# Attention with 16-feature heads: output in four quadrants of one PSUM bank, and one stage's TensorE, VectorE and ScalarE programs written out without a loop

## The reference, cut to what matters

```
# first layer (stage "Aatt"): causal, 16 heads
att = einsum('bhqd,bhkd->bhqk', q, k) / sqrt(16)
att = where(tril, att, -1e9);  att = softmax(att)
o   = einsum('bhqk,bhkd->bhqd', att, v)          # then @ W_proj + b_proj

# third layer (stage "Catt"): every query sees every key, with a bias per distance
att = einsum('bhqd,bhkd->bhqk', q, k) / sqrt(16) + compute_bias(rel_emb)
att = softmax(att)
o   = einsum('bhqk,bhkd->bhqd', att, v)          # then @ Wo
```

## Time and profile before

| | us |
|---|---|
| median of the runs | 7962.52 (three runs, 7954.46 to 7972.70) |
| the profiled execution, its own time | 7959.56 |
| its span in the profile | 7957.9 |
| from the start of `Aatt`'s products to its end, about | 280 to 1045 |
| from the start of `Catt`'s products to its end, about | 3150 to 4345 |

### The profile page before, as it was taken

How to read it: one execution, slowest core, us unless ns; L and a number is a source line. 1 busy time by engine, 2 the same in 40 slices (tenths; PEclk the granted TensorE clock), 3 DMA queues, 4 the chain that set the end, 5 groups by cost and what they waited for, 6 DMA issues and landing times. The chain is left out here.

```text
span 7957.9 us, 122287 instructions
## 1 busy us (share of the span) xinstructions
PE 6620.0 (83%) x30596; PEld 3410.1 (43%) x30596; DVE 4763.3 (60%) x12029; ACT 2802.6 (35%) x6066; POOL 1320.0 (17%) x779
## 2 busy tenths in 40 slices
PE   6799958989987966989988357996997788898979
PEld 2333334655455533222222244333554445544555
DVE  5655547733763634877775764996334675347635
ACT  0255524712462200555554111552110256124611
POOL 1110106100610003000000000551001441006100
PEclk9899989999998987999999678998998899999989
DMA  5322244542455256222221322113322345324541
GB/s 176 106 60 58 56 118 147 185 141 60 146 173 171 77 204 192 67 68 63 60 68 48 107 84 75 37 36 115 75 64 70 118 154 169 123 78 151 174 144 55
DMA packets 930584, 850.14 MB, mean 107 GB/s; under 512 B 240136, under 2 KB 786912, under 8 KB 929952
## 3 DMA queue, kind: packets, MB, share of 16 engines
q1 hardware_dynamic: 500624, 522.99, 23.0%
q10 hardware_dynamic: 429568, 323.08, 13.1%
HBM read 503.10 MB, written 346.00 MB: 107 GB/s over the span
## 5 line engine op out<-in xcount | busy, mean ns | idle before, releaser
L1243 ACT ACTIVATE Catt_E<-Catt_t 128x512 f32<-128x512 f32 x1024 | 577.6, 596 | 505.3 <-DVE Catt_t L1206 307.9
L1180 DVE CUSTOM_DVE_ANT_0 Catt_S<-Catt_s,Catt_win 128x1024 f32<-128x1024 f32 x512 | 620.8, 1214 | 5.9 <-DMA Catt_win<-skewed 3.7
L1180 DVE CUSTOM_DVE_ANT_0 Aatt_S<-Aatt_s,Aatt_win 128x128 f32<-128x128 f32 (+7 forms) x512 | 377.1, 756 | 303.8 <-PE Aatt_s L1110 297.7
L1160 PE MATMUL Catt_o<-Catt_E,Catt_V 128*32 128x256 f32 (+1 forms) x3840 | 549.5, 405 | 0.0
L1243 ACT ACTIVATE Aatt_E<-Aatt_t 128x512 f32<-128x512 f32 (+3 forms) x768 | 354.7, 489 | 326.8 <-PE Aatt_t L1142 251.5
L1206 DVE TENSOR_TENSOR Catt_t<-Catt_t,Catt_near 128x256 f32<-128x256 f32 (+2 forms) x640 | 281.7, 456 | 268.1 <-PE Catt_t L1139 234.6
L1139 PE MATMUL Catt_t<-Catt_Q,Catt_K 123*128 123x512 bf16 x1024 | 328.8, 389 | 92.8 <-ACT Catt_E L1243 73.4
L1110 PE MATMUL Catt_s<-Catt_K,Catt_Q 96*128 96x512 bf16 x1024 | 325.3, 401 | 23.4 <-DMA Catt_K<-k_parts 12.3
L1160 PE MATMUL Aatt_o<-Aatt_E,Aatt_V 128*32 128x256 f32 (+2 forms) x2304 | 323.8, 388 | 0.0
L1160 PEld LDWEIGHTS Catt_o<-Catt_E,Catt_V 128*32 128x32 f32 x3840 | 180.5, 110 | 272.9 <-issue 185.6
L2336 PE MATMUL scan_cum<-scan_X,scan_upto 128*128 128x512 f32 x512 | 265.8, 609 | 25.1 <-DVE scan_X L2405 23.7
(11 more groups left out here) (721 smaller groups left out, 14605.8 us busy)
## 6 DMA issues: line engine op xcount, KB each, us to landing
moe_cb<-c_s SPq DMA_DIRECT2D x16, 1024.0 KB, 10.5
bias_rows<-line SPq DMA_DIRECT2D x16, 960.0 KB, 6.3
skewed<-bias_win ACTq DMA_DIRECT2D x16, 960.0 KB
Catt_win<-skewed SPq DMA_DIRECT2D x16, 960.0 KB, 4.7
rec<-state_in_r ACTq DMA_DIRECT2D x32, 416.0 KB
scan_r<-rec SPq DMA_DIRECT2D x64, 208.0 KB, 2.5
Aatt_Q<-q_parts SPq DMA_DIRECT2D x32, 384.0 KB, 4.3
Aatt_K<-k_parts SPq DMA_DIRECT2D x32, 384.0 KB, 5.6
```

The lines of the kernel that those rows point to most:

```text
L1160: ins = t.matmul(o_ps[f:f + 2 * hd, x:y], V[:, b, kb, h, :], E[:, kb % NB, h, x:y], start=kb == 0, stop=kb == end and y == hi)
L1180: v.tensor_tensor_reduce(out=S[:, j % 2, 0:w], in0=s_ps[j % 2][:, 0:w], in1=win[:, 0 if causal else h, w0:w0 + w], scale=-1.0, scalar=BIG, ...
L1243: a.activation(E[:, kb % NB, h, lo:hi], t_ps[n % 2][:, 0:hi - lo], ACT.Exp, scale=scale).then_inc(exped, 1)
```

## The change: where o lies, the transfers around it, and the loop

One sequence's output now takes one bank whole: the 128-query blocks of a head are dealt in turn to two quadrants x = 0, 1, so that head h and parity x own the 32 partitions from (h * 2 + x) * 32 on, and 4 blocks of 128 columns in them. The other bank holds the next sequence. A full step has four products of 256 columns (two blocks with a stride), one per quadrant, where before it had two per quadrant in two quadrants. Only the first product of a quadrant in a bank starts the accumulation.

O and Rb are laid out alike ([128, B, 512] for [128, 2, 1024]), so ScalarE's copy and GpSimd's product become 128 by 512 for 64 by 1024. The sums leave in one transfer for two, the broadcast is one for two, and the store is four transfers with rows of 4 pieces of 512 bytes each, for two with rows of 4096 bytes.

`written_out` is new: the same order as `pipelined`, with all pairs written out and no loop. `Catt` uses it on TensorE, VectorE and ScalarE (`run`); `Aatt` keeps the loop on all engines, and SyncE and GpSimd keep it in both.

```diff
+def written_out(eng, count, steps, parts):
+    for i in range(count * steps + max(lag for lag, _ in parts)):
+        for lag, fn in parts:
+            if 0 <= i - lag < count * steps:
+                fn((i - lag) // steps, (i - lag) % steps)
...
     causal = bias is None
+    run = pipelined if causal else written_out
...
-        def half(x, b):
-            return x[b % 2 * 4 * hd:(b % 2 + 1) * 4 * hd, b // 2, :]
+        def quadrant(h, x):
+            return (h * 2 + x) * 2 * hd
...
-                    o = half(O, b)
-                    g.tensor_tensor(o, o, half(Rb, b), ALU.mult).then_inc(o_scaled, 1)
+                    g.tensor_tensor(O[:, b, :], O[:, b, :], Rb[:, b, :], ALU.mult).then_inc(o_scaled, 1)
...
-                step = CH if kb == 0 else 2 * P
-                for x in range(lo, hi, step):
-                    y = min(x + step, hi)
+                blocks = E[:, kb % NB].rearrange("p h (k x w) -> p h x k w", x=2, w=P)
+                for x in range(2):
+                    k0, k1 = (lo // P + 1 - x) // 2, (hi // P + 1 - x) // 2
+                    if k0 == k1:
+                        continue
                     for h in range(2):
-                        f = (b % 2 * 2 + h) * 2 * hd
-                        ins = t.matmul(o_ps[f:f + 2 * hd, x:y], V[:, b, kb, h, :], E[:, kb % NB, h, x:y],
-                                       start=kb == 0, stop=kb == end and y == hi)
+                        f, o = quadrant(h, x), b % 2 * CH
+                        ins = t.matmul(o_ps[f:f + 2 * hd, o + k0 * P:o + k1 * P], V[:, b, kb, h, :], blocks[:, h, x, k0:k1, :],
+                                       start=kb == 0 and c == 0, stop=c == 1 and kb == (NT - 2 + x if causal else NT - 1))
...
-                a.activation(half(O, b), o_ps[b % 2 * 4 * hd:(b % 2 + 1) * 4 * hd, :], ACT.Copy).then_inc(o_moved, 1)
+                a.activation(O[:, b, :], o_ps[:, b % 2 * CH:(b % 2 + 1) * CH], ACT.Copy).then_inc(o_moved, 1)
...
-                for h in range(2):
-                    f = (b % 2 * 2 + h) * 2 * hd + hd
-                    a.dma_start(sums[:, b % 2, h, :], O[f:f + 1, b // 2, :].rearrange("o (p c) -> o p c", c=NT)
-                                ).then_inc(sums_in[b % 2], 16)
+                a.dma_start(sums[:, b % 2, :], O[hd:P:2 * hd, b, :].rearrange("x (p c) -> x p c", c=2 * NT)
+                            ).then_inc(sums_in[b % 2], 16)
...
                 for h in range(2):
-                    f = (b % 2 * 2 + h) * 2 * hd
-                    a.dma_start(oT_s[bass.ds(it * (2 * hd) + h * hd, hd), b * T:(b + 1) * T], O[f:f + hd, b // 2, :]
-                                ).then_inc(o_out[b], 16)
+                    rows = oT_s[bass.ds(it * (2 * hd) + h * hd, hd), b * T:(b + 1) * T].rearrange("r (k x w) -> x r k w", x=2, w=P)
+                    for x in range(2):
+                        f = quadrant(h, x)
+                        a.dma_start(rows[x], O[f:f + hd, b, :].rearrange("r (k w) -> r k w", w=P)).then_inc(o_out[b], 16)
```

More of the change, by code:

```diff
@@ L981, in stage_thin_attention @@
         E = pl.sb("E", [P, NB, 2, T])
-        O, Rb = pl.sb("O", [P, 2, T]), pl.sb("Rb", [P, 2, T])
-        sums = pl.sb("sums", [P, 2, 2, NT])
+        O, Rb = pl.sb("O", [P, B, CH]), pl.sb("Rb", [P, B, CH])
+        sums = pl.sb("sums", [P, 2, 2 * NT])
         nmax, rest = pl.sb("nmax", [P, 2, 2, NT]), pl.sb("rest", [P, 2, NT])
@@ L1091, in _ @@
                 for b in range(B):
[L1092 removed]
+                    g.wait_ge(r_in[b % 2], it * 32 + (b // 2 * 16 + 16))
                     apart(g, pl.pool_unread)
[L1094 to L1095 removed]
+                    g.tensor_tensor(O[:, b, :], O[:, b, :], Rb[:, b, :], ALU.mult).then_inc(o_scaled, 1)
         @block.tensor
@@ L1153, in values @@
                 t.wait_ge(exped, it * nt + (n + 1 + PRIMED))
-                end = NT - 1 if c or not causal else NT // 2 - 1
-                step = CH if kb == 0 else 2 * P
-                for x in range(lo, hi, step):
-                    y = min(x + step, hi)
+                blocks = E[:, kb % NB].rearrange("p h (k x w) -> p h x k w", x=2, w=P)
[3 more added lines that the diff above has]
+                        continue
                     for h in range(2):
-                        f = (b % 2 * 2 + h) * 2 * hd
-                        ins = t.matmul(o_ps[f:f + 2 * hd, x:y], V[:, b, kb, h, :], E[:, kb % NB, h, x:y],
-                                       start=kb == 0, stop=kb == end and y == hi)
+                        f, o = quadrant(h, x), b % 2 * CH
+                        ins = t.matmul(o_ps[f:f + 2 * hd, o + k0 * P:o + k1 * P], V[:, b, kb, h, :], blocks[:, h, x, k0:k1, :],
+                                       start=kb == 0 and c == 0, stop=c == 1 and kb == (NT - 2 + x if causal else NT - 1))
                 ins.then_inc(pv_done, 1)
-            pipelined(t, PAIRS, ST, ((0, scores), (3, turn_maxima), (LAG, scores_by_key), (LAG + 3, values)))
+            run(t, PAIRS, ST, ((0, scores), (3, turn_maxima), (LAG, scores_by_key), (LAG + 3, values)))
         @block.vector
@@ L1211, in invert @@
                 b = i // GS
-                v.wait_ge(sums_in[b % 2], it * 64 + (b // 2 * 32 + 32))
+                v.wait_ge(sums_in[b % 2], it * 32 + (b // 2 * 16 + 16))
                 apart(v, pl.dve_unread)
                 v.reciprocal(sums[:, b % 2], sums[:, b % 2]).then_inc(inverted, 1)
-            pipelined(v, PAIRS, ST, ((LAG, add_near), (0, mask), (LAG + 9, invert)))
+            run(v, PAIRS, ST, ((LAG, add_near), (0, mask), (LAG + 9, invert)))
         @block.scalar
@@ L1224, in _ @@
             for i in range(B):
-                a.sem_inc(o_out[i], 32)
+                a.sem_inc(o_out[i], 64)
             def move_maxima(it, j):
@@ L1263, in write_sums @@
                 a.wait_ge(inverted, it * B + (b + 1))
-                a.dma_start(r_s[bass.ds(it * B + b, 1), :].rearrange("o (h p c) -> (o p) h c", h=2, c=NT), sums[:, b % 2]
+                a.dma_start(r_s[bass.ds(it * B + b, 1), :].rearrange("o (p c) -> (o p) c", c=2 * NT), sums[:, b % 2]
                             ).then_inc(r_out, 16)
@@ L1272, in spread_sums @@
                 a.wait_ge(o_scaled, it * B + (b + 1))
-                for h in range(2):
-                    f = (b % 2 * 2 + h) * 2 * hd
-                    a.dma_start(Rb[f:f + 2 * hd, b // 2, :], r_s[bass.ds(it * B + b, 1), h * T:(h + 1) * T].to_broadcast([2 * hd, T])
-                                ).then_inc(r_in[b % 2], 16)
+                row = r_s[bass.ds(it * B + b, 1), :].rearrange("o (x c) -> (o x) c", x=4)
+                a.dma_start(Rb[:, b, :], row.unsqueeze(1).to_broadcast([4, 2 * hd, CH])
+                            ).then_inc(r_in[b % 2], 16)
             def store(it, i):
```

7 lines of the change are left out of this document (3 added, 4 removed).

## The result

| | before | after |
|---|---|---|
| median of the runs, us | 7961.18 (7954.46 to 7972.70) | 7718.07 (7715.76 to 7726.33) |
| ratio, with its 95% interval | 1 | .9695 (.968 to .971) |
| `Aatt`, start of its first product to that of the next stage | 773.5 | 718.0 (-55.6) |
| `Catt`, the same | 1198.3 | 996.5 (-201.8) |
| all other stages together | 5986 | 6000 (+14) |

The kernel became 243 us faster; the forecast was 228. The page of after, to set beside the earlier trace rows: busy us of all engines, and the clock granted to TensorE in 40 slices.

What follows compares the result with a forecast made beforehand. TensorE was taken to set the pace in Catt and Aatt. Terms -105 (Catt), -77 (Aatt), -46 (edges) and 0 (ScalarE, transfers) sum to -228, so 7959.56 becomes 7732 us; range 7645 to 7905, 8 times in 10.

Steps and rivals of the forecast that it cites:

- Four quadrants at once: TensorE's o products: eight instructions take two rounds where they took four, .43 us less in each full step.
- The `Catt` step: Catt's steps: half of VectorE's .42 us idle time is gained, .21 us over some 500 steps, -105 us (-50 to -190).
- VectorE becomes the bound: In Catt, TensorE's part of a step falls to 1.72 us, where VectorE's busy time lies (1.73).
- the round of t: Catt: each of t's two banks goes from product to add to exponential to product, near 1.7 us with signals.
- The edges: Catt's six loop edges, 7.6 us each, go when written out: -46 us, gain between 31 and 50.
- The register instructions that go were beside other work: Catt's loop: removing its register instructions was given no gain of its own.
- `Aatt`: Aatt's steps: 36 blocks per (pair, b) become 20 rounds; 70% of 109 us taken, -77 us (-35 to -109).
- ScalarE and the store: ScalarE's queue: savings on copy, sums and broadcast offset two more store issues; 0, within 30 us.
- rival 3: TensorE's granted clock falls in much of both stages; with 40% of steps slow, about 8040 us; chance .06.
- Later stages: Stages after these are not touched, but their loops' edge stalls may gain or lose some: within 15 us.

Runs made afterwards that it cites:

- The kernel with two at a time: Changed kernel with Catt's even-block products before scores_by_key and odd-block ones behind it, never more than two quadrants at once: 7890.1 us, ratio .9919.
- spreading it: Changed kernel with the store's four transfer issues placed one by one in four successive steps: 7679.8 us, ratio .9649.
- doubled store: Changed kernel with each of the four store transfers issued a second time, to an unread HBM scratch, in both stages: 7941.7 us.

## Why the prediction was right, and where it was only nearly so

- **Four quadrants at once: right.** o is followed by s after .57 us (foreseen: .56). The kernel with two at a time shows that this is the whole of it. The estimate from the page of the Trainium skill, TensorE: Matmul & The Clock Gate, Part 3, would keep .54 us for the eight instructions and .11 around them, .65; the trace decides for full rounds, .46 and .11.
- **The `Catt` step: the size near, the cause wrong.** The term was -105. With the loop kept, the quadrants gave 119.7; without it, 143.6 (from 1140.1 to 996.5). The step that failed is "VectorE becomes the bound", with half of its idle time left over. VectorE is busy for 93% and still isn't the bound; the round of t, which the prediction had worked out as near 1.7 and then only used as a reason for taking half, is 1.68 and sets the step. TensorE's part of a steady step fell from 1.96 to 1.53, the round stayed, and the step went down to the round. The likeliest value would have been 1.68 for a steady step and 1.82 with the split (29.1 us for 16), not 1.94.
- **The edges: right in kind, short in size.** Forecast -46; 57 in the kernel before, 64 by the whole kernel and 82 by the stage with the quadrants (`moe` took back 9 of the 18 between). The step without an edge, 2.15 us, had been read inside the loop, so what the loop costs between its edges was left out. "The register instructions that go were beside other work" held for the steady steps, and only while TensorE was the bound.
- **`Aatt`: -55.6 for -77.** Without a drop of the clock a pair fell from 91.4 to 83.2 us, so 2.05 for each (pair, b), where 2.46 was foreseen: the store's four issues in a row stand in it, which cost some .6 in all, of which before's two may have had a part. That makes 64 us for the eight pairs (the first one, with little o, gives 6.3). The drops behind four edges took back 1.5 each, and the long store with its drop near 389 us 4: 54. The prediction had no term for the loop that `Aatt` keeps, which costs 26 us now. In the kernel before, the third step behind an edge takes 2.42 to 2.48 us, as in every other block of 16; in the changed one it takes 2.8 to 3.5 for 2.0 to 2.1 elsewhere (at the first edge the first two steps are longer instead).
- **ScalarE and the store: "0, within 30" held for `Catt` only.** There the fourth issue ends at 3653.75, and the adds for which the next exponential waits at 3653.64: it just fits. In `Aatt` the store costs mostly .6 to .9 us, which spreading it shows; how much of that the two issues of before had cost no run takes apart. The doubled store shows what lay behind the edge of that fit.
- **The clock: rival 3 was not the case, but its mechanism exists.** In `Catt` the granted clock stayed at 1.00 over 701 us. In `Aatt`'s loop it fell from 1.00 to .98, with drops behind edges and behind one long store, and in the doubled store to .85.
- **Later stages: within 15, at +14.** `moe` took 7.7 us more, `H0att` 5.0, the state's input 4.2, `B1att` 2.6. Their code is the same; the 8 us of `moe` recur in every kernel with `Catt` alone written out, the others are within what these stages differ by from kernel to kernel.

The sum came out 15 us short because the errors had both signs: the quadrants and the edges brought 51 us more in `Catt`, `Aatt` 21 less, and the other stages took 14. That the total came so near is in part luck.

## What to carry to other kernels

When the busiest engine is relieved, look for the longest round of signals through a buffer, not only for the next busiest engine: its length is there in the trace of before, and the step falls to it. What was free beside the old bound (register instructions ahead of waits, a row of transfer issues on an engine's queue) has to be priced anew once that round sets the pace; put issues one by one behind work that leaves the engine idle. Take the price of a loop from steps outside it, since steps inside pay too. Write out the hot loops where there is room, and take the time of unchanged loops as uncertain by some 15 us a stage when code ahead of them changes.

## What the runs showed of the hardware that was not expected

The same loop of the same code had stalls of 5 to 6 us at its edges in one kernel (`B1att`, 259.8 us) and none in another (244.3), depending on what stands ahead of it; 128 instructions more on VectorE made no difference. A register instruction of .035 us on ScalarE between an add and its exponential lengthened that gap from .03 to .11 us, and with it the round of three engines. And eight issues in a row on ScalarE's queue (3.9 us from 3662.80 to 3666.68, the store shown) cost 224 us in 56 places, 4.0 us each, with TensorE's granted clock falling behind each pause.
